# A two-block vision tower on one core: mixer powers for all pairs at once, clearing transfers spread over retention, the gating bias added one stage earlier, ranks in two matmuls

## The reference

```python
# token mixer: a kernel of 256 steps per channel from a diagonal state space model
dt = jnp.exp(log_dt)
A = -jnp.exp(inv_A_real) + 1j * A_imag
dtA = A * dt[:, None]
dA = (1.0 + dtA / 2) / (1.0 - dtA / 2)
V = jnp.exp(jnp.log(dA)[:, :, None] * jnp.arange(256))
K = 2.0 * jnp.einsum('chn,hnl->chl', C * B[None], V).real
# block 0
h = concatenate([cls_tok, K])
h = h + retention(layernorm(h)) @ Wout
u = layernorm(h)
x = u + causal_attention(layernorm(u, ln1)) @ Wp + bp
h = h + x + moe(layernorm(x, ln2))
# block 1: stable attention, then experts picked by product keys
```

## Time and profile before

| | us |
|---|---|
| runs of the kernel before, median (lowest to highest of 3) | 4756.81 (4755.84 to 4758.91) |
| the profiled execution's own time | 4754.65 |
| its span in the profile | 4752.8 |
| PE busy | 3820.0 (80%) |
| DVE busy | 2451.1 (52%) |
| ACT busy | 1567.9 (33%) |
| POOL busy | 326.3 (7%) |

### The profile page before, as it was taken

The page is one execution under the profiler, slowest core; times in us unless marked ns, Lnnn a source line. Parts: engine busy times, 40 slices in busy tenths (PEclk is TensorE's granted clock), DMA queues, the critical chain, the costliest instruction groups (busy, mean ns, idle before and its releaser), DMA issues. The chain is left out here.

```text
span 4752.8 us, 94621 instructions
## 1 busy us (share of the span) xinstructions
PE 3820.0 (80%) x38224; PEld 2748.7 (58%) x38224; DVE 2451.1 (52%) x6959; ACT 1567.9 (33%) x2605; POOL 326.3 (7%) x451
## 2 busy tenths in 40 slices
PE   1249946998886899993688777765999999999999
PEld 1236634656554777773344333334877777787776
DVE  8626654542234000003456344427887888888881
ACT  0013312225500323221221788852333333333331
POOL 0011111000024000004100000000000000000000
PEclk8569968999955999996789777866999999999997
DMA  1282142001133545443200000020000000000000
GB/s 33 55 349 83 25 134 78 20 21 32 26 105 104 202 167 186 166 179 120 73 15 15 14 15 18 16 90 28 9 9 15 9 9 15 9 9 15 9 5 5
DMA packets 162688, 295.59 MB, mean 62 GB/s; under 512 B 36688, under 2 KB 138944, under 8 KB 154480
## 3 DMA queue, kind: packets, MB, share of 16 engines
q1 hardware_dynamic: 122720, 199.73, 13.7%
q10 hardware_dynamic: 33296, 73.37, 4.0%
q0 software_dynamic: 6272, 16.85, 1.1%
HBM read 184.17 MB, written 105.20 MB: 61 GB/s over the span
## 5 line engine op out<-in xcount | busy, mean ns | idle before, releaser
L2272 PE MATMUL peer_total<-peer_up,peer_hid 128*128 128x256 f32 (+1 forms) x2112 | 566.0, 395 | 0.0
L2250 PE MATMUL peer_work<-peer_xnT,peer_down 128*128 128x256 f32 (+1 forms) x2176 | 558.4, 380 | 0.0
L2250 PEld LDWEIGHTS peer_work<-peer_xnT,peer_down 128*128 128x128 f32 x2176 | 410.6, 196 | 74.1 <-ACT peer_hid L2303 21.4
L2303 ACT ACTIVATE peer_hid<-peer_work 128x256 f32<-128x256 f32 (+1 forms) x544 | 202.6, 372 | 710.6 <-PE peer_work L2250 710.6
L2272 PEld LDWEIGHTS peer_total<-peer_up,peer_hid 128*128 128x128 f32 (+1 forms) x2112 | 376.5, 187 | 66.8 <-issue 15.3
L2323 ACT ACTIVATE peer_G<-peer_scat 128x512 f32<-128x512 f32 x258 | 272.3, 1056 | 261.5 <-PE peer_scat L2210 261.5
L2421 DVE TENSOR_TENSOR peer_hid<-peer_hid,peer_G 128x256 f32<-128x256 f32 (+1 forms) x544 | 216.3, 407 | 272.1 <-ACT peer_hid L2303 264.1
L1960 DVE TENSOR_TENSOR moe_yb<-moe_bank,moe_w 128x512 f32<-128x512 f32 x40 | 27.7, 692 | 624.1 <-PE moe_bank L1750 624.1
L2210 PEld LDWEIGHTS peer_scat<-peer_one_j,peer_one_i 64*64 64x64 f32 x16448 | 275.3, 138 | 123.2 <-issue 123.0
L1738 PE MATMUL moe_bank<-moe_xgT,moe_w 128*128 128x256 f32 x1280 | 295.2, 384 | 52.0 <-ACT moe_mid L1817 45.7
L2210 PE MATMUL peer_scat<-peer_one_j,peer_one_i 64*64 64x32 f32 x16448 | 302.6, 223 | 36.5 <-DVE peer_one_j L2400 14.6
(11 more groups left out here) (361 smaller groups left out, 6320.7 us busy)
## 6 DMA issues: line engine op xcount, KB each, us to landing
moe_w<-in_moe_w SPq DMA_DIRECT2D x40, 2180.0 KB, 8.7
ys<-ret_zeros ACTq DMA_DIRECT2D x16, 2296.0 KB, 52.5
moe_xg<-xs SPq DMA_DIRECT2D x40, 256.0 KB, 8.7
ys<-moe_yb ACTq DMA_DIRECT2D x40, 256.0 KB, 9.0
soft_xT<-xT SPq DMA_DIRECT2D x32, 257.0 KB, 2.8
stable_xT<-xT SPq DMA_DIRECT2D x32, 257.0 KB, 2.8
ret_xT<-xT SPq DMA_DIRECT2D x16, 257.0 KB, 2.8
aT<-ret_cN SPq DMA_DIRECT2D x64, 64.2 KB, 2.1
```

The lines of the kernel that those rows point to most:

```text
L2250: last = mm(work[:, jj % 2, 0:nb], down[:, c, jj, :], xnT[:, g % 3, c, 0:nb], start=c == 0, stop=c == DC - 1)
L2272: last = mm(total[:b_rows, j, :], hid[:, e % NHID, j * P:j * P + b_rows], up[:, e, :], start=e == 0 and j == 0, stop=e == JB - 1, skip_gro ...
L2303: A(hid[:, jj % NHID, 0:nb], work[:, jj % 2, 0:nb], ACT.Gelu).then_inc(gelu_ready, 1)
```

## The change

1. In `token_mixer` the parameters and `c_ri` of all 128 pairs are loaded once, and the 55 small operations are made once on tiles of 128x128. A turn takes its 32 pairs from them (`mine`) and begins with V. The loops are written out; `B_ri` and `c_ri` have a semaphore of their own, `weights_in`; the class token goes behind the loads on SP.
2. In `retention` each clearing transfer is issued by ACT in the turn of one entry, ahead of what it does at `s == SLOTS`.
3. `enter_attention` loads `soft_bp`, adds it to x on DVE (`xb`), makes `hx` from the sum and stores the sum as x.
4. `experts` has no bias matmul and no `bp` load any more, and `ranks` works on the four tiles of a group at once.

```diff
@@ token_mixer
-        par = r.sb("par", [P, 5, PC])
-        c_ri = r.sb("c_ri", [P, 2, PC, B])
+        par = r.sb("par", [P, 5, PAIRS])
+        c_ri = r.sb("c_ri", [P, 2, PAIRS, B])
...
-            sp.dma_start(cls[:, :], cls_tok[0:1, :].broadcast_to([B, D])).then_inc(cls_in, 16)
-            sp.wait_ge(cls_in, 16)
-            sp.dma_start(h_out[:, 0, :], cls[:, :]).then_inc(cls_out, 16)
             sp.sem_inc(stored, 16)
-            def load(t):
-                sp.wait_ge(inputs_free, t + 1)
...
+            for h2 in range(2):
+                half = slice(64 * h2, 64 * h2 + 64)
+                sp.dma_start(par[half, 0, :], log_dt[h2:h2 + 1, :].broadcast_to([64, PAIRS])).then_inc(loaded, 16)
+            sp.dma_start(par[:, 1, :], inv_A_real).then_inc(loaded, 16)
+            sp.dma_start(par[:, 2, :], A_imag).then_inc(loaded, 16)
+            sp.dma_start(par[:, 3:5, :], B_ri).then_inc(weights_in, 16)
+            sp.dma_start(c_ri[:, :, :, :], C_ri).then_inc(weights_in, 16)
...
+            dve.wait_ge(loaded, 64)
...
             def turn(t, parity):
-                dve.wait_ge(loaded, (t + 1) * 96)
...
+                mine = slice(t * PC, t * PC + PC)
                 dve.wait_ge(products_done, t + 1)
...
-                    e = [E[:, c, k, :].rearrange("p (a b) -> p a b", b=1).broadcast_to([P, PC, n]) for c in range(2)]
+                    e = [E[:, c, k, mine].rearrange("p (a b) -> p a b", b=1).broadcast_to([P, PC, n]) for c in range(2)]
...
+                if t == 0:
+                    dve.wait_ge(weights_in, 32)
...
-            with dve.Fori(0, turns // 2) as n:
-                turn(2 * n, 0)
-                turn(2 * n + 1, 1)
+            for t in range(turns):
+                turn(t, t % 2)
@@ retention, ACT
             act.wait_ge(zeros_made, 2)
-            for k in range(FILLS):
-                act.dma_start(blank[:, k, :], zeros[:, :]).then_inc(filled, 16)
...
                 for s in range(HEADS):
+                    if "B" in stages and s == SLOTS:
+                        act.dma_start(blank[:, bass.ds(g, 1), :].rearrange("p o n -> p (o n)"), zeros[:, :]).then_inc(filled, 16)
@@ enter_attention
+            sp.dma_start(next_b[:, :], next_b_in.broadcast_to([P, D])).then_inc(const_in, 16)
...
-                v.tensor_tensor(hx[:rows, q, 0:tiles, :], h1[:rows, q, 0:tiles, :], x[:rows, q, 0:tiles, :], ALU.add)\
+                bias = next_b[:rows, :].rearrange("p (a d) -> p a d", a=1).broadcast_to([rows, tiles, D])
+                chain.link(v.tensor_tensor(xb[:rows, q, 0:tiles, :], x[:rows, q, 0:tiles, :], bias, ALU.add))
+                v.tensor_tensor(hx[:rows, q, 0:tiles, :], h1[:rows, q, 0:tiles, :], xb[:rows, q, 0:tiles, :], ALU.add)\
                     .then_inc(rows_ready, 1)
...
-                act.dma_start(tokens(x_out, t0, tiles, rows), x[:rows, q, 0:tiles, :]).then_inc(rows_stored[q], 16)
+                act.dma_start(tokens(x_out, t0, tiles, rows), xb[:rows, q, 0:tiles, :]).then_inc(rows_stored[q], 16)
@@ experts
-            sp.dma_start(bp[:, :], bp_in.broadcast_to([P, D])).then_inc(const_in, 16)
...
-                        mm(proj[q][:rows, j, :], aT[:, q, c, j * P:j * P + rows], wp[:, c, :], start=c == 0, stop=False)
-                    last = mm(proj[q][:rows, j, :], ones[0:1, :rows], bp[0:1, :], start=False, stop=True)
+                        last = mm(proj[q][:rows, j, :], aT[:, q, c, j * P:j * P + rows], wp[:, c, :], start=c == 0, stop=c == DC - 1)
...
-                for j in range(tiles):
-                    mm(rank[:rows, j, :], before[:rows, :rows], both[:rows, g % 2, j, :], start=True, stop=False)
-                    last = mm(rank[:rows, j, :], ones[:, :rows], seen[:, g % 2, j, :], start=False, stop=True)
-                last.then_inc(rank_ready, 1)
+                n, flat = tiles * EXPERTS, "p j e -> p (j e)"
+                mm(rank_row[:rows, 0:n], before[:rows, :rows], both[:rows, g % 2, 0:tiles, :].rearrange(flat), start=True, stop=False)
+                mm(rank_row[:rows, 0:n], ones[:, :rows], seen[:, g % 2, 0:tiles, :].rearrange(flat), start=False, stop=True)\
+                    .then_inc(rank_ready, 1)
```

More of the change, by code:

```diff
@@ L201, in store @@
                         p0 = 64 * h2 + B * a
-                        dst = h_out[:, bass.ds(1 + h2 + t * (2 * PC), PC, 2), L1 * a:L1 * a + L1]
+                        first = 1 + h2 + t * (2 * PC)
+                        dst = h_out[:, first:first + 2 * PC - 1:2, L1 * a:L1 * a + L1]
                         sp.dma_start(dst, res[p0:p0 + B, :, :]).then_inc(stored, 16)
-            load(0)
-            with sp.Fori(0, turns - 1) as t:
-                load(t + 1)
+            sp.dma_start(cls[:, :], cls_tok[0:1, :].broadcast_to([B, D])).then_inc(cls_in, 16)
+            sp.wait_ge(cls_in, 16)
+            sp.dma_start(h_out[:, 0, :], cls[:, :]).then_inc(cls_out, 16)
+            for t in range(turns):
                 store(t)
-            store(turns - 1)
             sp.wait_ge(stored, 16 * 8 * turns + 16)
@@ L225, in copy_out @@
                 nc.scalar.activation(res[:, :, :], acc[:, :, :], ACT.Copy, scale=2.0).then_inc(res_ready, 1)
-            exponential(0)
-            with act.Fori(0, turns - 1) as t:
-                exponential(t + 1)
+            for t in range(turns):
                 copy_out(t)
-            copy_out(turns - 1)
         @block.vector
         def _(dve):
-            nc.vector.memset(prod[:, :, 0:1], 0.0).then_inc(inputs_free, 1)
             v = nc.vector
+            chain = Chain(dve, chained)
+            link = chain.link
             def products(chain, x, er, ei, n):
@@ L300, in turn @@
                     link(v.tensor_tensor(V[:, 1, :, n:2 * n], q[2], q[3], ALU.add))
[L302 to L303 removed]
+                if t == 0:
+                    dve.wait_ge(weights_in, 32)
+                bb = [par[:, 3 + c, mine].rearrange("p (a b) -> p a b", b=1).broadcast_to([P, PC, B]) for c in range(2)]
+                q = products(chain, [c_ri[:, c, mine, :] for c in range(2)], bb[0], bb[1], PC * B)
                 v.tensor_tensor(W[:, 0, :, 0, :], q[0], q[1], ALU.subtract)
@@ L317, in turn @@
                 dve.wait_ge(powers_ready, t + 1)
-                chain.done()
-            with dve.Fori(0, turns // 2) as n:
-                turn(2 * n, 0)
-                turn(2 * n + 1, 1)
+            for t in range(turns):
+                turn(t, t % 2)
         @block.tensor
@@ L340, in turn @@
                 last.then_inc(products_done, 1)
-            with pe.Fori(0, turns // 2) as n:
-                turn(2 * n, 0)
-                turn(2 * n + 1, 1)
+            for t in range(turns):
+                turn(t, t % 2)
 def groups(engine, step):
@@ L1608, in experts @@
         G = MOE_STEPS
-        N_CONST = 8
+        N_CONST = 7
         def at_tiles(g):
```

114 lines of the change are left out of this document (51 added, 63 removed).

## The result

| | us |
|---|---|
| kernel before, median of 4 | 4757.86 |
| changed kernel, median (4578.60 to 4618.10, 4 executions) | 4600.09 |
| ratio, with its 95% interval | 0.9665 [0.9619, 0.9711] |
| profiled execution of the changed kernel, own time | 4591.92 |
| its span | 4590.1 |

The forecast was 4612 in a range of 4597 to 4640. The middle of the four lies in it, 12 us under the forecast, but the four lie 40 us apart, while those of before lie 8 apart. That spread is the second thing to explain. (One execution of the kernel with early loads, further down, took 6455.81 at a mean clock of 0.545, far from all others, and is left out of its ratio.) The first is where the time went, and for that the profiled executions are laid side by side. For each stage the table takes the start of one instruction in both traces (the view of a line, first or last start) and shows how much earlier it comes.

The account below looks back on a forecast made before the run. Four stages run in sequence, bound by DVE (mixer), ACT's queue (retention), store waits (soft attention entry) and PE at 0.50 clock (experts' entry). -41.6 - 26.6 + 1.7 - 78 = -144.5 from 4754.65, plus 2.2: 4612 us, range 4597 to 4640.

Parts of the forecast that it names:

- A, mixer: Token mixer on DVE: small-operation prefix paid once on 128x128 tiles, V at 23.1, four unrolled turns of 31.87; -41.6 us.
- B, clearing transfers: Retention's start: ACT no longer issues sixteen clearing transfers first; K copy -23.6, earlier `decay` -3; together -26.6 us.
- I take nothing: Retention's turns: each clearing transfer's issue hides in ACT's 3.34 us wait, so costs 0; the longest would cost 45.
- C: Entry to soft attention: one more constant on SP (+0.5), a DVE addition exposed only in the first group (1.2); +1.7 us.
- D: Experts' entry: without bias matmuls and six of eight rank matmuls, clock rises, turn 12.8 instead of 22.95; -78 us together.
- Transposes, ACT and gates stay at 6.3 to 6.9: Experts' entry: the work after the ranks keeps its time, taken as 6.4 of the forecast turn of 12.8 us.
- second rival: Transfers or another engine bound: experts' loads make turns 14.2 (+8.4), or clearing transfers slow retention (+16); 4616 to 4636; chance 0.12.
- first rival: Experts' entry: clock stays at 0.50, turn 16.0, this stage gains only -55.7, total 4634; chance 0.13.
- fourth rival: Retention: each clearing transfer holds ACT's queue until it lands, 11.6 us a turn, +185, total 4797; chance 0.03.

Follow-up runs that it names:

- kernel with early loads: Changed kernel with SP issuing the experts' entry loads of aT and acc without waiting for the normalised rows; ratio 0.9681 to the kernel before.
- 128-row bias: Kernel before, with the experts' entry bias matmul made over 128 rows (ones in the first, zeros below) instead of one; 4700.51 against 4756.88, ratio 0.9884.

## Why the prediction was right

**The place of each term.** All four stood where the prediction put them: a DVE prefix paid once, an ACT queue that held the first K copy, a DVE addition in the shadow of a store, and a clock kept down by one-row matmuls. The single parts show each on its own: in their own stages -41.4, -33.1, -69.9 for the bias and -18.7 for the ranks. They do not simply add up: with the +1.5 of the new addition they make -161.6, and together they gave -144.5; 12 of the difference lie in the experts' entry and 5 in retention, as said above.

**A, mixer.** -41.6 forecast, -41.4 measured. Start at 4.53 for 4.9, V at 22.89 for 23.1, the end at 150.77 for 150.6. The pace of a wide operation, taken between rows of the two shapes, was right to 0.01 us.

**B, clearing transfers.** -26.6 forecast, -28.0 in the changed kernel and -33.1 alone. `decay` landed in 11.1 instead of 14.6, and PE's start came 3.5 sooner beside the 41.1 that the mixer had given, forecast 3. The step "I take nothing" for the issues was right: the longest took 0.368 in a wait of 3.34, where the 6.167 on record would have cost 45.

**C.** +1.7 forecast, +1.5 measured.

**D.** -78 forecast, -76.6 measured, but the working was not. The step that failed is "Transposes, ACT and gates stay at 6.3 to 6.9": at 2.4 GHz they take 1.07, 1.54 and 1.95, some 4.5 with their gaps. The ranks took 0.36 instead of 0.8. So PE's own chain takes 10.0 to 11.4 a turn, not 12.8, and the turn would have fallen to POOL's 11.3. It did not, since the `acc` load arrives late: PE waits 0.77 to 3.89 ahead of five projections. The forecast had that load at 13.0 into the turn, named it as next, and called it near enough. That is the load half of the second rival. Five waits of 10.6 together are 1.8 a turn, and 12.2 less 1.8 leaves 10.4 for PE: two errors, -2.4 and +1.8 a turn, nearly cancelled; a forecast of the early-load kernel made from the same working (six turns of 12.8 instead of 11.3) would have been off by 9 us. Two more errors cancelled around the turns. The six turns gave 64.4 (1354.69 to 1492.44 before, 73.33 now), 3.5 more than forecast. Behind them the entry gave 1.0 instead of 4.7: in the two short steps PE now waits 2.78 and 3.42 for DVE (0.84 and 3.49 before), and from their end to the first hidden matmul it now takes 38.0 instead of 35.4, waiting 26.89 for the gathered rows and 7.91 for the experts' weights (25.77 and 6.31 before). So the size of D was in part luck; its mechanism, the clock without one-row tiles, was not.

**The first rival** (clock at 0.50 in the entry) fell with 0.78. The reason that was given for it, that 25 us of busy PE had not raised the clock, was a reading of busy time; the 128-row bias shows that busy time was not the point. A PE that was busy in 25.22 of 25.30 us with one-row tiles among its work stayed at 1.2 GHz, and the same work with full tiles ran at 2.4 GHz (1.00 from 1322.73 to 1330.10). By the Trainium skill (TensorE: Matmul & The Clock Gate, Part 1) activity releases the throttle; the trace agrees for the full tiles alone.

**The fourth rival** (an issue holds the queue until its transfer lands) fell: the longest issue is 0.368, the shortest landing 7.1. The transfer half of the second rival (retention's turns longer by up to 1 us) fell as well, with turns of 17.77 against 17.78.

**What was not in the sum.** Stages without an edit were set at 0. The stable attention, from its first matmul to the first of the product keys, took 1018.8 before, 1024.5 after and 1018.3 to 1027.6 in the other profiles: an amount that moves by itself. The last group of the product keys adds nothing or 21 us and more (the two clusters lie 30 apart in the mean, 4587 and 4618). The kernel before ended at 0.50 in its profile and was never under 4746 in any comparison, the changed one ended at 1.00 in four of nine executions by their times. The forecast, made from a profile that ended at 0.50, is 4612, and the five executions that by their times ended so have 4608 to 4625. Why the unchanged group never stayed at 1.00 in the kernel before and did so in part of the executions of the changed one remains open; only that full tiles end it in both is shown.

## What to carry to other kernels

When a stage runs at the lower clock although PE is busy, look for matmuls with few rows or columns among its work before counting passes: taking away, or filling, four one-row matmuls a turn was worth more than their own time (-56 from filling alone, with nothing removed). When a term makes an engine faster, recompute every part of the turn at the new clock, not only the part that was edited, and then ask which load is due at the new time. And before a median of a kernel with a small last group is read, look at the clock of that group: it made 21 of the 163 us between the two profiles here.

## What was not expected of the hardware

- A bias matmul with one row kept PE at 1.2 GHz for a whole stage; with 127 rows of zeros added it runs at 2.4 GHz, and a tile falls from 3.15 to 1.29 us. At 0.50 the full form takes 2.69, so it is the cheaper one even without the clock.
- In a group whose first matmul moves 16 columns and whose second has 16 stationary ones the granted clock stayed at 1.00 in three profiles (the changed kernel twice and the one with early loads) and fell to 0.50 in six (the kernel before, its four single parts and the 128-row bias), with the same instructions in the group. Filling the second alone left it at 0.50 (4562.7 to 4592.7), filling both kept it at 1.00.
- Sixteen transfers of 2296 KB issued back to back took up to 6.167 us to issue; one per turn of 17.8 took 0.34 each, and landed after 10.0 instead of 52.5 (medians).
